# Up products of two chunks kept, levels and a third of the gated products moved to POOL

## The reference, cut to what matters

```python
def act_qdq(x):                       # one scale over the WHOLE tensor
    scale = max(max(abs(x)) / 32767, 1e-12)
    return clip(round(x / scale), -32768, 32767) * scale
n    = act_qdq(layernorm(y))
up   = act_qdq(n @ dq(w_up).T)        # 256 -> 768 features
gate = act_qdq(n @ dq(w_gate).T)
sig  = clip(round(sigmoid(gate) * 65536), 0, 65535) / 65536
gate = act_qdq(gate * sig)
o    = act_qdq(gate * up)
out  = y + tanh(g_ffn) * (o @ dq(w_down).T)
```

## Time and profile before

| | us |
|---|---|
| median of 3 runs (614.8 to 617.37) | 616.76 |
| the profiled execution, device time | 616.58 |
| its span, first to last instruction | 614.74 |

### The profile page before, as it was taken

How to read it: one execution, slowest core, us unless ns; L and a number is a source line. 1 busy time by engine, 2 the same in 40 slices (tenths; PEclk the granted TensorE clock), 3 DMA queues, 4 the chain that set the end, 5 groups by cost and what they waited for, 6 DMA issues and landing times. The chain is left out here.

```text
span 614.7 us, 11698 instructions
## 1 busy us (share of the span) xinstructions
PE 564.1 (92%) x4315; PEld 339.9 (55%) x4315; DVE 493.8 (80%) x835; ACT 439.0 (71%) x632; POOL 207.5 (34%) x227
## 2 busy tenths in 40 slices
PE   2679999899999999999987899999999899949998
PEld 1345666566665666666445444444444344438887
DVE  5788889999999988998828599979988799954442
ACT  2237888678787777887766354549999998869860
POOL 4723347766666879755345000000000000010100
PEclk9889999999999999999999799999999999969999
DMA  6523344455544444433241000000000000023443
GB/s 192 133 87 116 102 127 130 120 144 134 144 132 138 125 132 127 119 81 106 66 116 53 2 1 1 0 1 1 1 1 0 1 0 1 1 69 104 138 138 103
DMA packets 42812, 48.98 MB, mean 80 GB/s; under 512 B 10436, under 2 KB 30532, under 8 KB 42756
## 3 DMA queue, kind: packets, MB, share of 16 engines
q1 hardware_dynamic: 40916, 43.38, 24.2%
q0 software_dynamic: 1408, 4.46, 2.6%
q10 hardware_dynamic: 432, 0.39, 0.3%
HBM read 24.32 MB, written 8.70 MB: 54 GB/s over the span
## 5 line engine op out<-in xcount | busy, mean ns | idle before, releaser
L872 DVE TENSOR_REDUCE negm<-s_ps 128x2 f32<-128x512 f32 x256 | 163.5, 682 | 25.2 <-PE s_ps L516 24.5
L695 ACT ACTIVATE pt<-st_ps 128x512 f32<-128x512 f32 x256 | 138.9, 596 | 54.8 <-PE st_ps L531 53.8
L1205 PE MATMUL pairs<-xq,wut 128*128 128x512 f16 x576 | 124.7, 379 | 2.7 <-ACT lnall L1357 1.6
L1205 PEld LDWEIGHTS pairs<-xq,wut 128*128 128x128 f16 x576 | 56.2, 98 | 71.1 <-issue 2.3
L516 PE MATMUL s_ps<-kst,qst 96*128 96x256 f16 x512 | 81.0, 274 | 11.0 <-DVE negm L872 7.6
L531 PE MATMUL st_ps<-qst,kst 97*128 97x512 f16 x256 | 76.5, 379 | 1.5 <-DMA qst<-mrow 0.9
L455 PE MATMUL pv_ps<-pt,vt 128*32 128x256 f32 x1024 | 68.5, 385 | 0.6 <-ACT pt L695 0.6
L1645 POOL PARTITION_ALL_REDUCE vmax<-vmax x5 | 1.8, 357 | 194.8 <-DVE vmax L1464 119.8
L516 PEld LDWEIGHTS s_ps<-kst,qst 96*128 96x128 f16 x512 | 46.0, 98 | 33.3 <-DVE negm L872 23.1
L1205 PE MATMUL pairs<-xq,wgt 128*128 128x512 f16 x276 | 60.5, 379 | 0.0
L1280 PE MATMUL pairs<-wdt,h 128*128 128x256 f16 x384 | 49.4, 281 | 8.4 <-ACT h L1393 8.4
(11 more groups left out here) (207 smaller groups left out, 1047.4 us busy)
## 6 DMA issues: line engine op xcount, KB each, us to landing
qst<-qk SPq DMA_DIRECT2D x96, 64.0 KB, 2.1
kst<-qk SPq DMA_DIRECT2D x45, 128.0 KB, 3.2
xt<-in_x SPq DMA_DIRECT2D x16, 256.0 KB, 4.3
ct<-in_ctx SPq DMA_DIRECT2D x16, 256.0 KB, 2.9
xr<-in_x SPq DMA_DIRECT2D x16, 256.0 KB, 3.9
out<-y SPq DMA_DIRECT2D x16, 256.0 KB, 3.8
lnall<-out POOLq DMA_DIRECT2D x8, 512.0 KB, 4.3
recb<-rec_dram SPq DMA_DIRECT2D x15, 256.0 KB
```

The costliest lines, as they stand in the source:

```text
L695: nc.scalar.activation(pt[:, (j // 2) % 2, j % 2, kt], st_ps[u % 3][:], ACT.Exp, scale=1.0 / (WS * WS * HD ** 0.5)).then_inc(exp_done, 1)
L872: nc.vector.tensor_reduce(negm[:, b % 2, tt, lo:lo + 5:4], s_ps[tt][:], AX.X, ALU.max, negate=True).then_inc(max_done, 1)
L1205: mm = nc.tensor.matmul(ps[:, p, k, :], w[:, a, dt, f * P:(f + 1) * P], xq[:, b, c, dt, :], start=n == 0, stop=n == len(terms) - 1)
```

## The change

- **Block scales spread.** SCALES holds six steps for each weight: three reduces, then the scale, its reciprocal and its multiple, each at a step of its own. The clip of a weight (L964) comes one step later.
- **Levels.** For the first seven chunks ACT makes the levels of tile 0 only, for the last chunk those of tiles 0 and 1. POOL makes the rest in f32 and in place in gb, in two tensor_scalar instructions of 128 x 1024: times 65536 plus 2^23, then minus 2^23 with a minimum. `gated` reads them from there. The order on DVE is turned: `gated(c-1, p)` now stands ahead of `up_max(c, p)`.
- **Two chunks kept.** ACT copies the up tiles of chunks 2 and 5 from PSUM to SBUF (`keep_up`), one after the chunk's sigmoid, two after its level tile. `up_max` of these chunks reads the copy, and PE waits for the copy (u_kept) where it waited for the maximum. The second pass goes in ORDER 2, 0, 1, 5, 3, 4, 6, 7, and PE computes again only the six chunks that were not kept.
- **A third of six chunks on POOL.** For the first six chunks in ORDER, tile 2 is multiplied by POOL with four instructions of 128 x 1024: times K2 (a tensor_tensor with a broadcast column), rounding by adding and subtracting 1.5 x 2^23, the same subtraction for the up tile (which ACT writes in f32 with that number added, into `uf`), and the product. DVE takes its maximum.
- **Unread products.** 6 matmuls at the end of attention and 24 after the second pass write to PSUM and nobody reads them.
- Some semaphores are merged or dropped.

```diff
-    SCALES = (2, 34, 66)
+    SCALES = ((-3, -2, 5, 5, 6, 6), (21, 22, 29, 30, 37, 38), (54, 61, 62, 69, 70, 71))
@@ attention, TensorE, after the matmul that spreads the value
+            for _ in range(6):
+                nc.tensor.matmul(s_ps[0][:].rearrange("p a b -> p (a b)"), wo2[:, 0, 0, 0:P],
+                                 wo2[:, 0].rearrange("p a b -> p (a b)"), start=True, stop=True)
@@ attention, VectorE
-                for i, n in pieces_behind(g, 4):
+                for i, steps in enumerate(SCALES):
+                    for p in range(PARTS):
+                        if g == steps[p]:
+                            part_scales(i, p)
+                    if g == steps[3]:
+                        scale_of_blocks(i)
+                    if g == steps[4]:
+                        inverse_of_blocks(i)
+                    if g == steps[5]:
+                        step_of_blocks(i)
+                for i, n in pieces_behind(g, 5):
@@ feed_forward
+    KEPT = (2, 5)
+    ORDER = (2, 0, 1, 5, 3, 4, 6, 7)
+    POOLED = 6
+    AGAIN = [c for c in ORDER if c not in KEPT]
+        def pools(n, p):
+            return p == PR - 1 and n < POOLED
+        def own_before(n):
+            return PR * n - min(n, POOLED)
+        def level_tiles(c):
+            return 1 if ahead(c, 1) else PR - 1
@@ TensorE
+                    if c - 1 in KEPT:
+                        pe.wait_ge(u_kept, kept_before(c - 1) + p + 1)
+                    else:
+                        pe.wait_ge(u_max, PR * c + p + 1)
                     products(wut, c, p).then_inc(u_done, 1)
...
+            pe.wait_ge(p3_done, own_before(NC) - 2)
+            spare_products(ps[:, 3, 1], 24)
@@ ScalarE
+            def keep_up(c, p):
+                act.wait_ge(u_done, PR * c + p + 1)
+                nc.scalar.copy(kept_up[KEPT.index(c)][:, 2 * p:2 * p + 2], ps[:, p]).then_inc(u_kept, 1)
...
+                if c in KEPT:
+                    keep_up(c, 0)
                 act.wait_ge(sig_done, c + 1)
-                for p in range(1 if ahead(c, 1) else PR):
+                for p in range(level_tiles(c)):
...
+                if c in KEPT:
+                    for p in range(1, PR):
+                        keep_up(c, p)
                 if ahead(c, 1):
                     gate_int(c + 1, 1 - d)
...
+            for n in range(2, NC):
                 for p in range(PR):
+                    if pools(n - 2, p):
+                        act.wait_ge(p3_pool, n - 1)
+                    else:
+                        act.wait_ge(p3_done, own_before(n - 2) + p + 1)
+                    if not pools(n, p):
+                        gate_integers(n, p)
+                    up_integers(n, p)
@@ VectorE
                 for p in range(PR):
+                    gated(c - 1, (c - 1) % 2, p)
                     up_max(c, p)
-                    if p == 0:
-                        dve.wait_ge(sq_done, c)
-                    gated(c - 1, (c - 1) % 2, p)
             dve.wait_ge(u_max, PR * NC + PR)
             whole(1, PR * NC)
+            for p in range(PR - 1):
+                gated(NC - 1, (NC - 1) % 2, p)
             dve.wait_ge(all_max, 3)
             scale(vmax[:, 1, 1:2], UX, VX, SU, KU)
...
+            gated(NC - 1, (NC - 1) % 2, PR - 1)
...
+            ready = (0, 0)
+            for n in range(NC):
+                for p in range(PR):
+                    if (n, p) != (0, 0) and not pools(n, p):
+                        products(n, p)
+                        product_max(*ready)
+                        ready = (n, p)
+                        if p == 1 and n and pools(n - 1, PR - 1):
+                            product_max(n - 1, PR - 1)
+            product_max(*ready)
@@ POOL
+            def levels(c, p, n):
+                pool.wait_ge(sig_done, c + 1)
+                tile = gb[:, c, 2 * p:2 * p + 2]
+                nc.gpsimd.tensor_scalar(tile, tile, LEVELS, WHOLE, ALU.mult, ALU.add).then_inc(sums_done, 1)
+                pool.wait_ge(sums_done, n + 1)
+                nc.gpsimd.tensor_scalar(tile, tile, WHOLE, LEVELS - 1.0, ALU.subtract, ALU.min).then_inc(levels_done, 1)
...
+            def pool_product(n):
+                c = ORDER[n]
+                tile = gb[:, c, FT - 2:FT].rearrange("p f w -> p (f w)")
+                nc.gpsimd.tensor_tensor(tile, tile, col(K2).broadcast_to((P, 2 * CW)), ALU.mult).then_inc(sums_done, 1)
+                pool.wait_ge(sums_done, LEVELED + 3 * n + 1)
+                nc.gpsimd.tensor_scalar(tile, tile, SIGNED, SIGNED, ALU.add, ALU.subtract).then_inc(sums_done, 1)
+                pool.wait_ge(qu_done, PR * n + PR + PR)
+                nc.gpsimd.tensor_scalar(uf[:, n % 2], uf[:, n % 2], SIGNED, None, ALU.subtract).then_inc(sums_done, 1)
+                pool.wait_ge(sums_done, LEVELED + 3 * n + 3)
+                nc.gpsimd.tensor_tensor(tile, tile, uf[:, n % 2], ALU.mult).then_inc(p3_pool, 1)
```

More of the change, by code:

```diff
@@ L1170, in ahead, with kept_before, sq_before @@
             return c + k < NC
+        def pools(n, p):
+            return p == PR - 1 and n < POOLED
+        def own_before(n):
+            return PR * n - min(n, POOLED)
+        def kept_before(c):
+            return PR * sum(k < c for k in KEPT)
+        def level_tiles(c):
+            return 1 if ahead(c, 1) else PR - 1
+        def sq_before(c):
+            return sum(level_tiles(k) for k in range(c))
         last_half = ps[:, 0, 0, 0:D]
@@ L1207, in products, with spare_products @@
                 return mm
+            def spare_products(bank, n):
+                for _ in range(n):
+                    nc.tensor.matmul(bank, wgt[:, 0, 0, 0:P], wgt[:, 0, 0, 0:CW], start=True, stop=True)
             first_turn()
@@ L1433, in units_of @@
                 units[0] += 2
+            nc.vector.memset(col(MAGIC), SIGNED).then_inc(magic_set, 1)
             dve.sem_inc(u_max, PR)
@@ L1583, in _ @@
             products(0, 0)
-            for n in range(1, PR * NC - 1):
-                products(n // PR, n % PR)
-                product_max((n - 1) // PR, (n - 1) % PR)
-            product_max(NC - 1, PR - 2)
-            products(NC - 1, PR - 1)
-            product_max(NC - 1, PR - 1)
+            ready = (0, 0)
[8 more added lines that the diff above has]
+            product_max(*ready)
             dve.wait_ge(p3_max, PR * NC)
@@ L1645, in over_partitions @@
                 nc.gpsimd.partition_all_reduce(vmax[:, i, 1:2], vmax[:, i, 0:1], P, RMAX).then_inc(all_max, 1)
-            nc.gpsimd.partition_all_reduce(warm[:], t["lmaxall"][:], P, RMAX).then_inc(warmed, 1)
-            for n, i in enumerate((0, 4, 1, 2, 3)):
-                over_partitions(n, i)
+            nc.gpsimd.partition_all_reduce(warm[:], t["lmaxall"][:], P, RMAX)
+            over_partitions(0, 0)
+            def levels(c, p, n):
[4 more added lines that the diff above has]
+                nc.gpsimd.tensor_scalar(tile, tile, WHOLE, LEVELS - 1.0, ALU.subtract, ALU.min).then_inc(levels_done, 1)
+            n = 0
+            for c in range(NC):
+                if c == 1:
+                    over_partitions(1, 4)
+                for p in range(level_tiles(c), PR):
+                    levels(c, p, n)
+                    n += 1
+            over_partitions(2, 1)
+            over_partitions(3, 2)
+            LEVELED = PR * NC - sq_before(NC)
+            def pool_product(n):
+                c = ORDER[n]
+                tile = gb[:, c, FT - 2:FT].rearrange("p f w -> p (f w)")
[6 more added lines that the diff above has]
+                nc.gpsimd.tensor_tensor(tile, tile, uf[:, n % 2], ALU.mult).then_inc(p3_pool, 1)
+            pool.wait_ge(chain, 2 + 3 + 3 + 3)
+            for n in range(POOLED):
+                pool_product(n)
+            over_partitions(4, 3)
+            pool.wait_ge(p3_pool, POOLED)
             def body(c, d):
```

116 lines of the change are left out of this document (71 added, 45 removed).

## The result

The changed kernel took 686.51 us (median of 4 runs, 684.75 to 687.85) against 615.78 for the kernel before, run beside it: a ratio of 1.1146, 95% interval 1.1101 to 1.1192. The forecast was 624.3, with a range up to 636: the sign was right, but a rise of 7.7 was forecast and one of 70.7 measured. The profiled execution has a span of 685.9 us, 71.2 more than before.

A forecast was written before the change was run, and what follows sets the result against it. ScalarE was taken to bound the sigmoid stage, VectorE and TensorE to tie in the second pass, TensorE to bound the down stage. 616.6 - 2.0 - 1.9 + 6.0 + 7.1 - 1.5 = 624.3 us; whole range 602 to 636.

The forecast's parts named there:

- Part 1: Price of a one-input constant tensor_scalar on POOL at 128x1024: 1.07 us, bounds 0.96 and 4.3.
- Part 2: Memory port: a VectorE instruction with two SBUF inputs and a POOL instruction exclude each other for their whole length.
- rival C: POOL's constant tensor_scalar costs per element what the pointer form does, 4.3 us: about 740 us in all; chance 0.06.
- Part 4: Second pass: POOL is the bound at 8.8 us a pooled chunk, 64.4 against 57.3 us: +7.1, bounds -6 and +11.
- rival A: The memory port costs nothing where it matters, in sigmoid stage and second pass: 604.5 us; chance 0.28.
- Part 3: Sigmoid stage, walked chunk by chunk: 8.0 us an ordinary chunk, 12 a kept one; +6.0, bounds -0.7 and +9.
- the port: Second pass: VectorE needs the memory port twice per pooled chunk, 2 x 1.14 us, added to POOL's 6.4.
- Rival B: The memory port costs little: +2 in the sigmoid stage, +4 in the second pass, 617 us; chance 0.14.
- Part 5: The rest: spread scales -2.0 us, unread products at the end of attention -1.9, those before the down stage -1.5.

The follow-up runs named there:

- x1_swap: The kernel before plus one unread 128x1 instruction on POOL between two of its reductions: 625.87 us, ratio 1.0125.
- m1_forms: The kernel before plus unread POOL instructions of various forms on scratch tiles in the gate stage, where POOL idles: 620.15 us in its only run.
- e5: The changed kernel with POOL's one-input steps as multiply-then-add, one taking in the broadcast product, and the limit at 65535 left out: 634.51 us, ratio 1.0292.
- x2_turned_max: e5 with the three reductions in and behind the sigmoid stage moved from POOL to TensorE and VectorE: 627.59 us, ratio 1.0159.
- b0: The kernel before plus only the 24 unread products ahead of the down stage: 616.90 us, ratio 1.0001.
- e4_neither: The changed kernel with all levels back on ScalarE and no product of the second pass on POOL: 623.69 us, ratio 1.0112.
- b2: b0 with 38 unread products ahead of the down stage instead of 24: 616.06 us, ratio 0.9994 to the kernel before.

## Why the prediction was wrong, point by point

**The step that failed is in Part 1: "One input has less to read than either and more than the memset: I take 1.07".** The nearest row in shape was no near row in kind. For the one POOL form that is times-plus the value was right (1.03); for the three others the means are 3.69, 4.50 and 2.77, of which the form is 3.63, 3.63 and 2.77 (the rest of the 4.50 is in Part 2). The error is 2.6 us x 15 level tiles and 4.3 us x 6 pooled chunks, 64 us of POOL work on the engine that the same text found to be the bound of the second pass. The row that held the truth was in front of me: the normalising instruction, 1.254 us for 256 elements. I had made it the upper bound, and then charged its price to the pointers and gave it 6 in 100 as rival C. The upper bound of Part 4 (+11) even took the step at 1.4, so the range up to 636 did not hold the doubt that Part 1 had stated. Rival C was half right: a pair of operations that is not times-plus does cost nearly what it said (3.63 against 4.3), but it had times-plus at 4.3 too (1.03), and so 740 as the end.

**A term was missing: the changeover of POOL.** The sigmoid stage of the changed kernel pays it at 437.80 and 444.86 and again at 525.07, the second pass at 534.85: 6.0 + 6.7 + 6.2 + 6.7. x1_swap shows one pair by itself. "POOL does nothing else in stages 1 to 3" was a fact of the kernel before, and I did not ask what that was worth: the term stood at nothing. Nor did I ask what 11 us of "issue" ahead of its first reduction mean; m1_forms, which leaves that part alone, has the same idle, 11.22, in its first row above.

**Part 2, the exclusion, was right where POOL's instruction is quick**, also for int16 inputs, which rival A left open: e5 shows 1.04 to 1.89 and 1.22 to 2.04. In the changed kernel the quick instruction takes 1.81 on average instead of 1.03, 11.6 us over 15 tiles. It is not a law of whole instructions. VectorE and POOL in the changed kernel, in two chunks, and the product that ran when POOL's instruction at 536.83 (shown above) began:

```profile
422.24 3.67 POOL L1753 TENSOR_SCALAR gb<-gb 128x1024 f32<-128x1024 f32 x1
...
422.75 1.62 DVE L1623 CUSTOM_DVE_ANT_0 gb<-lnall 128x1024 f32<-128x1024 int16 x1
...
425.99 2.08 POOL L1751 TENSOR_SCALAR gb<-gb 128x1024 f32<-128x1024 f32 x1
...
428.16 3.62 POOL L1753 TENSOR_SCALAR gb<-gb 128x1024 f32<-128x1024 f32 x1
...
457.77 3.62 POOL L1753 TENSOR_SCALAR gb<-gb 128x1024 f32<-128x1024 f32 x1
...
457.84 2.04 DVE L1623 CUSTOM_DVE_ANT_0 gb<-lnall 128x1024 f32<-128x1024 int16 x1
...
535.00 2.81 DVE L1664 TENSOR_TENSOR gb<-lnall 128x1024 f32<-128x1024 int16 x1
```

Both gated products began and ended within a slow instruction, which took 3.67 and 3.62 with them and 3.62 alone. The one issued 0.07 us after the slow one's start took 0.8 longer than alone, the one issued 0.51 after it 0.4: a slow instruction keeps the product out for its first 0.9 us only. The other way round it is stopped like a quick one: the slow one at 536.83 began under a product that ran to 537.81 and took 4.51, and so did all six of its kind, where the same pair alone took 3.63 in m1_forms. The quick one at 425.99 took 2.08 beside a gated product. The Trainium skill's "SBUF — State Buffer", "Who interferes with whom", on which Part 2 leaned, has the holder keep the pair for the whole instruction (it says so of VectorE's 2-port modes); for the slow forms the measurement differs and decides. So rival A is false, and its price (604.5) with it.

**Part 3, the walk, ends in the right place once both causes are out of the way, in part by luck.** x2_turned_max has quick forms and no changeover in the stage. From the start of the first gate_int its sigmoids end at 5.7, 12.5, 20.5, 32.7, 39.6, 48.9, 61.1, 67.9; the forecast had 5.8, 12.4, 20.3, 32.1, 40.1, 48.1, 60.0, 68.0. No entry is off by more than 1.1. But single chunks are: the fifth takes 6.9 and the last 6.8 where 8.0 stood, the sixth 9.3, and these cancel. The tail was short: 11.7 us from there to the last scale instead of 9.2, as VectorE meets POOL in gated products still in hand (2.03 at 475.49 and 478.59) and the turned maximum takes 1.6 us to the scale, where POOL's took 0.5. With the real prices the walk does not apply: the stage is then POOL's own sum, 15 tiles at (1.03 or 2.08) + 3.65 and gaps = 4.8 or 5.9, and three changeovers.

**Part 4, the second pass, had the right structure and the wrong prices.** POOL is the bound, VectorE takes the sixth pooled tile's maximum and nine operations after it (four products and five maxima, where the forecast wrote three and six). A pooled chunk is 1.89 + 4.49 + 2.77 + 2.34 and a gap; of the 2.3 that the forecast added for the port, 0.9 was paid, inside the 4.49. The rows of the end:

```profile
604.54 1.22 DVE L1673 TENSOR_REDUCE cmax<-gb 128x1 f32<-128x1024 f32 x1 [5.30 <-POOL gb L1777]
...
613.59 2.34 DVE L1673 TENSOR_REDUCE cmax<-gb 128x1 f32<-128x1024 f32 x2
```

From the last scale at 528.8: 6.05 of changeover, 6 x 11.6, and 11.4 for ten operations make 87.1, and the last maximum ends at 615.9. With 8.8 for 11.6 and no changeover this is the 64.4 of the forecast. Rival B had put the point from which the edit pays at 7.6 us a pooled chunk. e5 is there, with 7.58, and its pass is still 5.7 us longer than before: 6.79 of changeover stand ahead of the first pooled tile.

**Part 5.** The down stage is 2.1 shorter (forecast -1.5) and 618 to 630 reads 1.00, but by luck. This is TensorE's row of the 24 unread products:

```profile
609.21 7.87 PE L1256 MATMUL pairs<-wgt 128*128 128x512 f16 x24 [11.29 <-DVE gb L1664]
```

TensorE had idled 11.29 us for the late second pass, so the products ran at a lowered clock, took 7.87 us instead of the forecast's 5.2, and reached to 617.1. Where they ran at full clock (5.3 us) they ended too early: b0 has 3.19 us of idle behind them, 0.72 and a stage of 69.8, e4_neither 4.85 us, 0.50 and 71.0, the length of before. In time over all b0 and b2 show nothing beyond their intervals, so the sign rests on the stage alone. In this profile the opening gained nothing: +0.7 where -3.9 stood. The matmuls after the six unread ones took 4.44 us for 12 against 4.89, but the part began 1.4 us later, 0.9 of it behind them. The start of that part varies by almost 7 us between the profiles of this study (338.0 to 344.7), so one pair says little. The seven profiles with the edits of the opening reach the sigmoid stage at 408.7 to 416.9, on average 412.7; the seven without at 412.8 to 417.7, on average 415.1. That is 2.4 less, about the size of the scatter: the gain is likelier than the +0.7 suggests, is not shown, and cannot be divided between scales and products.

As a sum of the profile: 614.7 + 0.7 + 42.7 + 29.9 - 2.1 = 685.9.

## What to carry to other kernels

Price an instruction by a row of its own kind of operation, not by one of its size: on this POOL, write one-input steps as multiply-then-add, also where the factor is 1.0, and count any other form at 2.7 to 3.9 times that (m1_forms). When work is put on an engine that so far did one kind of thing, ask what it costs to alternate, and try it with one tiny unread instruction, as x1_swap does; an unexplained "issue" idle in the old profile (7.5 us ahead of POOL's first tensor_scalar in the earlier trace rows, 11.2 ahead of its first reduction) is a reason to ask. When the one row of the right kind bounds a cost at four times the value taken, on the engine that will be the bound, that doubt is the forecast: here the form, with the broadcast product that it took in, was worth 52 us (e5).
